# A four-block transformer kernel with two mixture-of-experts layers: routing steps, weight splits, returned rows and scatters in another order

## The reference

```python
x = x + tanh(g_xattn[0]) * L0_xattn(layernorm(x), ctx)   # 16 heads of 64, LayerNorm inside, gated
x = x + tanh(g_ffn[0])   * L0_ffn(layernorm(x))          # 8 experts of 256 hidden, relu, top-2 of softmax
x = x + tanh(g_xattn[1]) * L1_xattn(layernorm(x), ctx)   # one head of 128
x = x + tanh(g_ffn[1])   * L1_ffn(layernorm(x))          # shared expert + 8 experts of 512 hidden, silu, top-2
```

## Time and profile before

| | |
|---|---|
| median of 3 runs | 302.24 us (301.48 to 303.0) |
| profiled execution | 301.93 us, its span 300.2 us |
| PE busy | 277.2 us (92%) |
| DVE busy | 192.3 us (64%) |
| ACT busy | 166.6 us (55%) |
| POOL busy | 96.3 us (32%) |

### The profile page before, as it was taken

One profiled execution on the slowest core, in us unless ns is written; L12 is line 12 of the kernel. 1 busy time (PEld: TensorE's weight loads), 2 busy tenths in 40 slices (PEclk: granted clock), 3 DMA queues, 4 the chain that ended last, 5 costly groups with the idle time before them and its releaser, 6 DMA issues.

```text
span 300.2 us, 6266 instructions
## 1 busy us (share of the span) xinstructions
PE 277.2 (92%) x2157; PEld 238.4 (79%) x2157; DVE 192.3 (64%) x607; ACT 166.6 (55%) x354; POOL 96.3 (32%) x144
## 2 busy tenths in 40 slices
PE   1999997899989978999998999999899999999995
PEld 0477875688878866888986898788779889999985
DVE  2797968488899988246758577635967722432106
ACT  2494349878867756332355553668626631566560
POOL 1167006468855542012016531100101430155610
PEclk9999999999999999999999999999999999999999
DMA  7692100099600000090000000000000245921122
GB/s 183 205 305 31 3 0 3 0 263 244 136 3 2 1 2 0 5 314 3 0 2 0 0 3 0 1 2 0 2 1 2 76 137 189 276 94 40 42 87 71
DMA packets 20526, 20.49 MB, mean 68 GB/s; under 512 B 2097, under 2 KB 15049, under 8 KB 20496
## 3 DMA queue, kind: packets, MB, share of 16 engines
q1 hardware_dynamic: 19088, 18.09, 21.2%
q0 software_dynamic: 1120, 1.88, 2.8%
q10 hardware_dynamic: 288, 0.13, 0.2%
HBM read 15.86 MB, written 4.24 MB: 67 GB/s over the span
## 4 chain that ended last, share of the span: by engine, by line
PE 65%; DVE 19%; POOL 5%; issue 4%; ACT 3%; DMA 2%; SPq 0%; DVEq 0%; ACTq 0%; POOLq 0%
PE bank L1252 10%; PE bank L1431 9%; PE bank L1225 7%; PE bank L1226 6%; PE bank L1227 6%; PE bank L1419 4%; PE bank L1412 4%; DVE xhat_sb L908 4%; PE bank L1210 4%; POOL p_sb L643 3%; DVE sum_sb L845 3%; PE bank L1170 3%; DMA ctx_tok_sb<-in_ctx 2%; PE bank L1181 2%; DVE negmax_sb L834 2%
## 5 line engine op out<-in xcount | busy, mean ns | idle before, releaser
L786 ACT ACTIVATE hT_sb<-bank,cols_sb 128x512 f32<-128x512 f32 x72 | 48.6, 689 | 52.8 <-PE bank L1227 52.4
L643 POOL TENSOR_TENSOR p_sb<-p_sb,recip_sb 128x480 f32<-128x480 f32 x32 | 31.6, 989 | 48.1 <-DVE recip_sb L848 48.1
L1147 DVE SCALAR_TENSOR_TENSOR x_sb<-bank,wts_sb,x_sb 128x128 f32<-128x128 f32 x96 | 27.0, 343 | 26.1 <-PE bank L1431 17.2
L1252 PEld LDWEIGHTS bank<-we_sb,hT_sb 128*128 128x128 f32 x320 | 37.1, 192 | 1.2 <-issue 0.5
L1252 PE MATMUL bank<-we_sb,hT_sb 128*128 128x128 f32 x320 | 38.0, 276 | 0.0
L695 POOL TENSOR_TENSOR rstd_sb<-veps_sb,minus_half_sb 128x4 f32<-128x4 f32 (+1 forms) x11 | 11.0, 999 | 66.9 <-DVE veps_sb L900 66.6
L1431 PE MATMUL bank<-w_sb,hT_sb 128*128 128x128 f32 x256 | 31.5, 276 | 0.0
L1431 PEld LDWEIGHTS bank<-w_sb,hT_sb 128*128 128x128 f32 x256 | 30.4, 192 | 1.2 <-issue 0.4
L796 ACT ACTIVATE p_sb<-bank,bias_t_sb 128x128 f32<-128x128 f32 x60 | 17.1, 371 | 16.3 <-PE bank L1412 16.3
L1181 PE MATMUL bank<-ident_sb,p_sb 128*120 128x128 f32 x128 | 19.7, 280 | 4.9 <-POOL p_sb L643 4.6
L686 POOL DMA_INDIRECT ys_hbm<-w_kv_sb,targets_sb x15 | 14.4, 960 | 25.9 <-DVE w_kv_sb L817 25.6
(11 more groups left out here) (217 smaller groups left out, 609.0 us busy)
## 6 DMA issues: line engine op xcount, KB each, us to landing
xs_hbm<-col_rows_sb SPq DMA_DIRECT2D x1, 2145.0 KB, 15.8
we_sb<-in_L_ffn_We SPq DMA_DIRECT2D x1, 2048.0 KB, 9.0
w_sb<-in_L_ffn_We SPq DMA_DIRECT2D x8, 256.0 KB, 3.1
w_after_sb<-in_L_ffn_We SPq DMA_DIRECT2D x7, 256.0 KB, 3.9
w_kv_sb<-in_L_xattn_w_kv SPq DMA_DIRECT2D x2, 512.0 KB, 6.9
w_sb<-in_L_ffn_w SPq DMA_DIRECT2D x1, 1024.0 KB, 11.0
w_kv_sb<-xs_hbm SPq DMA_DIRECT2D x15, 65.0 KB, 2.9
x_sb<-in_x SPq DMA_DIRECT2D x1, 512.0 KB, 7.4
```

Of the source, the lines that this page charges most:

```text
L643: nc.gpsimd.tensor_tensor(p0[j % 4], p0[j % 4], recip0[:, j % 2, :].unsqueeze(2) .broadcast_to([128, HG, SK]), ALU.mult).then_inc(probs_re ...
L786: nc.scalar.activation(hT[:, u % 2, c, :], ps(item)[:, :], ACT.Relu if n == 1 else ACT.Silu, bias=cols[:, col:col + 1]).then_inc(read(item ...
L1147: last = nc.vector.scalar_tensor_tensor(out=x[:, b, :], in0=ps(key)[:, C * i:C * (i + 1)], scalar=w, in1=x[:, b, :], op0=ALU.mult, op1=ALU ...
L1252: last = nc.tensor.matmul(ps(key)[:, C * i:C * (i + 1)], hT[:, unit_at[(n, p, e)] % 2, c, 128 * i:128 * (i + 1)], we2[:, e, c, :], start=( ...
```

## The change

The change edits the order of the list at four places, and two transfers.

First, in the last steps of the first attention (`first_done` is step 23) the routing of L0's first half moves: `logits` from behind `attend` 30 to behind `attend` 29, `top` from behind 31 to behind 32, `hot` from behind 32 to behind 33, where `weights` stays. Second, the nine splits of L1's weights, which stood one by one from the end of the first half's L0 experts on, move: six of them now stand with the routing of the second half (behind `logits 1 1`, `top 1 1`, `v1 0`, `hot 1 1`, `weights 1 1` and `k1 1`), ahead of `consts` and of `stats 2 0`; the other three are spread later. Third, `wT 3 0` moves from ahead of `o1 1` to behind `down 3 0 0`, which on PE is behind two of the four `up` products of unit (3, 0, 2). Fourth, `comb` moves ahead of `down 3 1 8` on DVE, and rows 4 to 7 of x are reported ready by that last sum and no longer by `comb`; the second half of the last unit gets one of banks 0 to 5 in place of 6 or 7.

The two transfers: the returned rows come in two loads of 256 KB with one semaphore, in place of eight of 64 KB with four; and each scatter waits for the one two ahead of it (same choice `k`, previous sequence) in place of each pair waiting for the pair before. SP holds back the first four loads of expert weights for the tiles until six of the eight scatters have landed.

```diff
-    spaced = dict(zip((0, 1, 4, 7, 8, 9, 10, 12), [("stats", 1, (HB // 2, HB)), ("xhat", 1, (HB // 2, HB)),
-                                                   ("xT", 1, 0), *route_items(1, 0)[:-1]]))
+    spaced = {0: [("stats", 1, (HB // 2, HB))], 1: [("xhat", 1, (HB // 2, HB))], 4: [("xT", 1, 0)],
+              6: [("logits", 1, 0)], 9: [("top", 1, 0)], 10: [("hot", 1, 0), ("weights", 1, 0)], 12: [("wT", 1, 0)]}
...
     rest = add_units(expert_units(0)[n_tail:], [[("stats", 1, 1), ("b2", 1, 0)]] + one_by_one(
-        [("xhat", 1, 1), ("k1", 0), ("xT", 1, 1), ("logits", 1, 1), ("top", 1, 1), ("v1", 0),
-         ("hot", 1, 1), ("weights", 1, 1), ("k1", 1), ("v1", 1), ("wT", 1, 1), ("b2", 1, 1)]))
-    chain = [[]] + attend1[0] + into_ff1
+        [("xhat", 1, 1), ("k1", 0), ("xT", 1, 1)]) + [[item, split] for item, split in zip(
+            [("logits", 1, 1), ("top", 1, 1), ("v1", 0), ("hot", 1, 1), ("weights", 1, 1), ("k1", 1)], splits)]
+        + one_by_one([("v1", 1), ("wT", 1, 1), ("b2", 1, 1)]))
+    chain = [[("consts",)]] + attend1[0] + into_ff1
     chain = [(rest[k] if k < len(rest) else []) + items for k, items in enumerate(chain)]
-    chain = [splits[k:k + 1] + items for k, items in enumerate(chain)]
-    chain[0] = [("consts",)] + chain[0]
+    for k, split in zip((6, 8, 13), splits[6:]):
+        chain[k] = chain[k] + [split]
...
-            [("wT", 3, 0), ("o1", 1), ("stats", 3, 1)],
-            [], [("xhat", 3, 1), ("b2", 3, 0)], [("xT", 3, 1)], [("r1", 1)],
+            [("o1", 1), ("stats", 3, 1)],
+            [("wT", 3, 0)], [("xhat", 3, 1), ("b2", 3, 0)], [("xT", 3, 1)], [("r1", 1)],
...
-    schedule.insert(-1, ("comb",))
+    summed = schedule.index(("down", *units[-2]))
+    schedule.insert(summed, ("comb",))
...
-            plan(part_key(item), 6 + downs % 2)
+            key = part_key(item)
+            plan(key, turn % 6 if key[0] == "down2" else 6 + downs % 2)
...
+            for k in range(2):
+                sp.wait_ge(scattered[k], 16 * (HB - 1))
             load_w1(range(0, TG))
-            sp.wait_ge(scattered, 16 * 2 * HB)
+            for k in range(2):
+                sp.wait_ge(scattered[k], 16 * HB)
...
-            for i in range(HB):
-                for k in range(2):
-                    at = HALF * k + 1 + 128 * i
-                    sp.dma_start(y_of[:, k, i, :], ys_hbm[at:at + 128, :]).then_inc(gathered[i], 16)
+            for k in range(2):
+                at = HALF * k + 1
+                sp.dma_start(y_of[:, k], ys_hbm[at:at + HALF, :].rearrange("(i p) c -> p i c", p=128)) \
+                    .then_inc(gathered, 16)
...
-                    else:
-                        pool.wait_ge(scattered, 16 * 2 * i)
                     for k in range(2):
+                        if i:
+                            pool.wait_ge(scattered[k], 16 * i)
                         pool.indirect_dma_start(
...
                 elif kind == "comb":
+                    dve.wait_ge(gathered, 16 * 2)
                     for i in range(HB):
                         b = HB + i
-                        dve.wait_ge(gathered[i], 16 * 2)
...
-                        last.then_inc(x_ready, 1)
+                    link(last)
...
-                        if item[1:] == units[-1]:
+                        if item[1:] in units[-2:]:
                             last.then_inc(x_ready, 1)
-                    if item[1:] != units[-1]:
+                    if item[1:] not in units[-2:]:
```

More of the change, by code:

```diff
@@ L171, in flamingo_kernel @@
         if i - first_done in spaced:
-            schedule.append(spaced[i - first_done])
+            schedule.extend(spaced[i - first_done])
         if i in (STEPS, STEPS + 2, STEPS + 4):
@@ L485, in flamingo_kernel @@
         xs_landed = [sem(f"xs_landed{j}") for j in range(TILES)]
-        scattered = sem("scattered")
-        gathered = [sem(f"gathered{i}") for i in range(HB)]
+        scattered = [sem(f"scattered{k}") for k in range(2)]
+        gathered = sem("gathered")
         tables_ready = sem("tables_ready")
@@ L679, in _ @@
                                 ap=slots[:, k, i:i + 1].bitcast(U32), axis=0),
-                            in_=xhat_wide[:, HB + i, :], in_offset=None).then_inc(scattered, 16)
+                            in_=xhat_wide[:, HB + i, :], in_offset=None).then_inc(scattered[k], 16)
                 elif item[0] == "dnt":
```

## The result

| | before | after |
|---|---|---|
| median (runs) | 302.62 us (4; 301.48 to 303.43) | 299.27 us (4; 298.84 to 299.59) |
| profiled span | 300.2 us | 297.5 us |

The ratio is 0.9898, with a 95% interval of 0.9868 to 0.9928: 1.0% faster, 3.1 us by the ratio (2.2 to 4.0 by the interval), 2.7 us by the two spans. The forecast was 299.6 us, a gain of 2.6.

What follows compares the result with a forecast made beforehand. PE, busy 92% of the span, was taken as the bound. Terms 2.7 + 1.1 - 1.9 + 0.7 gave 2.6 us gained, scatters nothing: 302.24 - 2.6 = 299.6 us, range 297.6 to 301.4.

Steps and rivals of the forecast that it cites:

- five terms: Attention's end 2.7 us gained, splits 1.1 gained, wT 3 0 1.9 lost, scatters nothing, the end 0.7 gained.
- first term: The end of the first attention, where moving the routing steps was to gain 2.7 us.
- Attention's end: First attention's last steps: logits earlier and top behind the sum shorten PE's three waits, 2.7 us gained.
- PE's own way to the last transposes: End of first attention: PE by itself reaches step 31's transposes at 116.9, leaving 0.2 us of waiting.
- The other chain: Step 31, first attention: maxima at 112.4, exponents 113.85, sum 115.0, product 115.95, transposes 117.1.
- Splits: Second attention's first transpose: with six splits done before, PE's 1.08 us wait for xhat 2 0 goes, 1.1 us gained.
- The delay feared for DVE beside the subtractions: Second half's routing: DVE's steps beside POOL's six moved splits delayed 0.5 to 1 us, not felt by wT 1 1's copy.
- `wT 3 0`: First half's L1 experts: o1 1 still starts at 211.78, b2 3 0 waits for DVE's late copy, 1.9 us lost.
- Scatters: Returned tokens' scatters: the last lands some 5 us earlier but nobody waits for it, so nothing is gained.
- The fourth rival: Scatters slow each other, pages come 5 us later, PE stands some 4.8 us: 304.4 us, chance 0.06.
- The end: After PE's last matmul: two loads and comb first let DVE end at 297.3 in place of 298.04, 0.7 us gained.
- 291.8: Kernel's end: assumed landing of the two loads of returned rows, between 290.4 and 293.4 us.

Runs made afterwards that it cites:

- e15: The kernel before with the scatters' edit alone, run a second time on the third chip: 302.01 us, ratio 0.9995.
- e6: The kernel before with only the scatters' waits and SP's hold on the first weight loads changed, on the second chip: 308.38 us.
- e3: The kernel before with only the routing steps of the first attention moved: 299.63 us, ratio 0.9919.
- e13: The changed kernel with the scatters' edit taken back, on the third chip: 300.60 us, ratio 0.9937.
- e7: The changed kernel with eight loads of the returned rows on one semaphore in place of two loads, second chip: 307.07 us, ratio 1.0176.
- e8: The changed kernel with the copy of pT1 1 ahead of the weights and wT 3 0 right behind o1 1, second chip: 303.04 us, ratio 1.002.
- e1: The changed kernel with wT 3 0 put back ahead of o1 1: 297.66 us, ratio 0.9845.
- e12: The changed kernel again, unaltered, on the third chip: 299.56 us, ratio 0.9919.

## Why the prediction was right

The time was 299.27 us against 299.6, the gain in the traces 2.65 us against 2.6, and the signs of the five terms and four of their mechanisms held as worked out; the first term was 0.3 us too large, for a wait that I had not seen. That the sum came so close is partly luck: 0.1 us each from the splits and `wT 3 0`, and 0.1 us that had been gained ahead of the first landmark, made up for the first term. The parts alone, by their ratios and with the scatters as on the third chip (`e15`), make -0.81 - 0.51 + 0.60 - 0.05 - 0.15 = -0.92%, the changed kernel -1.02%: within their intervals they add up. With the scatters as on the second chip (`e6`) they would not.

- **Attention's end**, 2.7 predicted, 2.4 in the trace, 2.5 alone. The gain of the logits' place and of `top` behind the sum came as worked out. The step that failed is PE's own way to the last transposes, put at 116.9: it had no wait for step 29's product, which the logits' new place on DVE delays. With those 0.61 us PE came at 117.24, and the 0.2 us of waiting predicted there fell away. `e3` has the same wait (0.60 us). I had cited the very rule for the splits and not applied it to L959. The other chain came out as forecast, by luck: the maxima (L838) came at 112.88 and not at 112.4, but I had carried over the 1.43 us between the start of the maxima and the exponents, and it was 0.91, since ACT's copy and not the maxima ends last there. So the exponents began at 113.79 (113.85 forecast), the sum at 114.94 (115.0), the product at 115.89 (115.95).
- **Splits**, 1.1 predicted, 1.2 in the trace, 1.5 alone (1.1 to 2.0 by the interval). `xhat 2 0` took the 1.12 us of `xhat 3 0`. The delay feared for DVE beside the subtractions was one line, L970, 0.4 us, and PE did not wait for it.
- **`wT 3 0`**, 1.9 lost predicted; 1.8 in the trace, 1.8 alone. Waits of 1.8 and 1.5 us were named, 1.83 and 1.40 came. Missed was that a stretch at half the clock can follow these idle times: in `e13`'s profile it cost 1.6 us.
- **Scatters**, nothing: right in the changed kernel's trace and on the third chip, wrong on the second. The fourth rival had the place and a loss of that order (4.8 us, then 304.4), but not the mechanism: the pages came early, and what stood was DVE and ACT. On that chip the changed kernel itself did not run; `e7`, which has all of it but the two loads, took 307.07.
- **The end**, 0.7 predicted, 0.70 in the trace, 0.5 alone. `comb` began 3.72 us behind the first load's issue; I had taken 291.8, which is 3.76 behind 288.04. That is luck, since 291.8 was only a value between two bounds, but any landing up to 292.2 gave the same end. The Trainium skill's figure for 1 MB (DMA: Bandwidth & Descriptors, Measured), which is for a transfer issued from GpSimd and from which I had estimated a landing near 292.5, was further off; and by my own working that landing gives 0.5 us of gain, not 0.4.

## What to carry to other kernels

Read an order of work by the last step ahead of each idle time of the bounding engine, and move what stands between that step and its input: `top` from between two sums, the copy of `pT1 1` from behind the weights. An item that is moved only behind its waiting predecessor adds an idle time and does not remove one. Test an edit that is off the critical path on more than one chip before keeping it: the scatters' edit gained nothing on the third chip and cost 1.8 to 7.6 us on the second.

## What the runs showed of the hardware

- With scatters 1.3 us apart, DVE and ACT of one chip stood idle for 3 to 8 us with no releaser that the trace shows (`e6`, `e7`, `e8`); in the other profiles with the same edit (the changed kernel's first, `e1`, `e12` and `e15`) never. The cause is open.
- PE's granted clock was 0.50 to 0.66 in stretches of 2 to 6 us behind idle times of 1.4 to 4.1 us, in some executions of a program and not in others. Such a stretch cost 1.6 us in `e13`'s profile and nothing in `e12`'s. What decides whether it comes, no run here shows.
- DVE operations of 0.16 to 0.19 us took 0.58 to 0.79 us beside a product or subtraction of POOL (L959, L970).
